# A sparse-and-dense key-value attention layer on one core: where the second dense pass of a tile stands

## What is computed

```python
x = x + relu(xn @ W_upd + (adj.T @ (xn @ W_msg)) / deg + bias)      # xn = layernorm(x)
q = (xn @ Wq) * 128 ** -0.5                                         # xn = layernorm(x) again
scores, index = product_keys(xn)            # top 16 of 128 on two sides, top 16 of the 256 sums
w = softmax(scores)                                                 # 16 weights per node and head
k = sum(w * keys_table[index]); v = sum(w * values_table[index])
x = x + softmax(causal(q @ k.T)) @ v @ Wo                           # 8 heads, float32
```

## Time and profile before

| what | value |
|---|---|
| time, median of 3 runs | 17072.46 us (17061.4 to 17086.94) |
| span of the profiled execution | 9595.0 us |
| that execution's own time outside its span | not given |
| median less span | 7477 us |
| PE busy | 8080.2 us, 84% |
| DVE busy | 7220.8 us, 75% |
| POOL busy | 6794.0 us, 71% |
| ACT busy | 4866.4 us, 51% |
| mean granted clock of TensorE | 0.888 |

### The profile page before, as it was taken

The page is one execution under the profiler, slowest core; times in us unless marked ns, Lnnn a source line. Parts: engine busy times, 40 slices in busy tenths (PEclk is TensorE's granted clock), DMA queues, the critical chain, the costliest instruction groups (busy, mean ns, idle before and its releaser), DMA issues.

```text
span 9595.0 us, 181229 instructions
## 1 busy us (share of the span) xinstructions
PE 8080.2 (84%) x51232; PEld 6240.2 (65%) x51232; DVE 7220.8 (75%) x32005; ACT 4866.4 (51%) x14163; POOL 6794.0 (71%) x7177
## 2 busy tenths in 40 slices
PE   5888888888888888888888888888888888888898
PEld 4666666666666766667666676666666666666676
DVE  7787777877777777777776777777777777877775
ACT  3555445455454554545445454454554545545454
POOL 5777767777677776777767777677776767767666
PEclk7899889998888998889888898898998989988898
DMA  4555445554454554545444454455554545545454
GB/s 126 166 171 161 155 154 162 163 162 158 155 160 158 162 165 150 160 157 166 158 152 158 159 164 157 155 162 161 164 165 150 166 151 165 167 150 160 146 167 138
DMA packets 445985, 1516.88 MB, mean 158 GB/s; under 512 B 123760, under 2 KB 141552, under 8 KB 379248
## 3 DMA queue, kind: packets, MB, share of 16 engines
q0 software_dynamic: 344064, 939.98, 32.5%
q1 hardware_dynamic: 100848, 564.37, 16.8%
HBM read 1499.66 MB, written 4.19 MB: 157 GB/s over the span
## 4 chain that ended last, share of the span: by engine, by line
PE 53%; DVE 36%; issue 5%; ACT 5%; DVEq 1%; DMA 0%; ACTq 0%; SPq 0%
PE dense_ps L470 20%; DVE wide L1114 10%; PE comb_ps L580 10%; PE wideT_ps L456 5%; PE front_ps L410 4%; DVE onehot L1005 4%; PE score_ps L446 4%; DVE chosen L1010 3%; DVE hits L1078 3%; DVE onehot L998 3%; PE score_ps L507 2%; PE score_ps L495 2%; PE probT_ps L513 2%; DVE neg L1131 1%; ACT expo L706 1%
## 5 line engine op out<-in xcount | busy, mean ns | idle before, releaser
L343 POOL DMA_INDIRECT got<-in_table,rows x7168 | 6792.1, 948 | 2778.2 <-issue 2203.5
L470 PE MATMUL dense_ps<-tab,wideT 128*128 128x256 f32 x16384 | 3959.9, 385 | 4.7 <-ACT kv_d L641 3.8
L470 PEld LDWEIGHTS dense_ps<-tab,wideT 128*128 128x128 f32 x16384 | 3002.5, 192 | 640.4 <-issue 274.7
L1114 DVE SCALAR_TENSOR_TENSOR wide<-const_ps,rank,expo 128x128 f32<-128x128 f32 x8192 | 2303.7, 344 | 1268.0 <-PE wideT_ps L456 993.1
L706 ACT ACTIVATE expo<-sim_d,shift 128x128 f32<-128x128 f32 x8192 | 2596.8, 393 | 118.0 <-DVE wide L1114 117.3
L641 ACT ACTIVATE wideT<-wideT_ps 128x512 f32<-128x512 f32 x2048 | 1212.0, 592 | 1070.2 <-PE wideT_ps L456 1065.8
L456 PE MATMUL wideT_ps<-ident,wide 128*128 128x128 f32 x8192 | 1237.1, 274 | 118.3 <-DVE wide L1114 61.0
L456 PEld LDWEIGHTS wideT_ps<-ident,wide 128*128 128x128 f32 x8192 | 1005.9, 141 | 386.0 <-DVE wide L1114 101.6
L580 PE MATMUL comb_ps<-got,spread 128*32 128x256 f32 x14336 | 1078.7, 452 | 4.8 <-DVEq L1102 4.0
L446 PE MATMUL score_ps<-group_of,lifted 128*128 128x16 f32 x1792 | 344.1, 329 | 554.3 <-DVE lifted L1021 554.3
L580 PEld LDWEIGHTS comb_ps<-got,spread 128*32 128x32 f32 x14336 | 481.5, 126 | 491.3 <-issue 299.5
(11 more groups left out here) (155 smaller groups left out, 8417.1 us busy)
## 6 DMA issues: line engine op xcount, KB each, us to landing
tab<-in_dense SPq DMA_DIRECT2D x512, 1024.0 KB
got<-in_table,rows POOLq DMA_INDIRECT x7168, 2.7
adj_i<-in_adj SPq DMA_DIRECT2D x16, 1024.0 KB, 9.6
x_in<-in_x SPq DMA_DIRECT2D x16, 256.0 KB
out<-fin SPq DMA_DIRECT2D x16, 256.0 KB, 6.0
tab<-in_wqpk_t SPq DMA_DIRECT2D x1, 512.0 KB, 11.0
tab<-in_keys_t SPq DMA_DIRECT2D x1, 512.0 KB, 15.5
wq_sb<-in_wq SPq DMA_DIRECT2D x1, 512.0 KB, 15.2
```

The costliest lines, as they stand in the source:

```text
L343: pool.indirect_dma_start(out=got[got_no(n)][:, g, :], out_offset=None, in_=table, in_offset=bass.IndirectOffsetOnAxis(ap=rows[:, t * GATH ...
L470: mm = pe.matmul(dense_ps[:, v * 2 * D:(v + 1) * 2 * D], wideT[k % 2][:, (2 * u + v) * P:(2 * u + v + 1) * P], tab[(k // CHUNK) % 2][:, (2 ...
L1114: last = dve.scalar_tensor_tensor(wide[k % 2][:, 2 * u + v, :], count_ps[:, v, :], rank1[:, 2 * half + v, key:key + 1], expo[k % 2][:, 2 * ...
```

## The change

The pass of place w[1] goes elsewhere on all three engines. On PE it stood between `key_transpose` and `scores` and now stands between `values` and `project`. On ACT it stood between the kv copy and `take_keyT` and now stands behind `take_headT`. On DVE it stood in front of the selection's second step and now stands behind w[4]. The plan's counts stay, so a slot has as many passes as before. DVE's `weigh` gets one wait more, at the first pass of each half: for its own last weighing, before the counts that this one reads are overwritten.

```diff
--- PE, batch
                 key_transpose(a, t, kv, kv_copied, slot + 1)
-                k = passes(b, k, w[1], first)
                 if t == 0:
                     pe.wait_ge(q_copied, s + 1)
...
                 values(a, t, kv)
+                k = passes(b, k, w[1], first)
                 project(a, h)
--- ACT, batch
                 copy(kv[:, t, :], comb_ps[:, 0:2 * D]).then_inc(kv_copied, 1)
-                k = passes(b, k, w[1], first, last)
                 take_keyT(a, t, keyT)
...
                 take_headT(a)
+                k = passes(b, k, w[1], first, last)
--- DVE, weigh
             if k % HALF_PASSES == 0:
+                dve.wait_ge(wide_ready, m)
                 after(link(dve.tensor_copy(count_ps, count_sb[:, :, :])))
--- DVE, batch
                 if half is not None and o == 2:
                     best_dense(half, 0)
-                k = passes(b, k, w[1], last)
                 hit_part(1)
...
                 k = passes(b, k, w[4], last)
+                k = passes(b, k, w[1], last)
                 if more and t % 2 == 1:
                     sum_rows(nt)
                     lift(m, t0, nt)
```

## The result

The changed kernel takes 16628.42 us (median of 4 runs, 16619.52 to 16643.95); beside it the kernel before took 17066.93. The ratio is 0.9742, 95% interval 0.9728 to 0.9756: 439 us less, where 194 had been forecast and 16710 was the low end of the range. The direction was right, the size not.

The account below looks back on a forecast made before the run. DVE was taken to set the end of odd slots, PE that of even ones. Gains of 150 + 4 + 40 = 194 us, with 7477 us outside the span held fixed, gave 17072 − 194 = 16878, say 16880; range 16710 to 17060.

Parts of the forecast that it names:

- the 7477 us: Gap between the profile's span of 9595 us and the median of 17072.46, taken as fixed and untouched by the change.
- step 3: Short slots n = 1, 2, 15, 16: moved pass against earlier negate, between 2 us less and 2 more each; taken as 0.
- Step 1: Even slots: PE's 0.37 us stall moves from project to scores; nothing gained, between 0 and 0.3 us worse per slot.
- Steps 2 and 4: Odd slots: DVE's wait for PE's turn goes, 10.0 us per batch; PE's clock drops less behind shorter waits, 2.6.
- the new wait that I looked for: Sign of being wrong: in odd slots DVE's moved weighing waits for PE's turn of w[4]; none expected in n = 9.
- Waits at the move: Sign of being right: PE's waits at L446 for DVE's lifted, 554.3 us in 194 waits, fall below 400 us.
- step 4: PE's clock after waits at the move: six places, a third helped, 2.6 us per batch, 40 us in all.
- rival (a): PE's clock stays up in all eight places, 204 us instead of 40: 16714 us; chance 0.12.
- rival (d): Slower: the moved pass runs at low clock in the four short slots, costing 222 us: 17197 us; chance 0.12.
- Step 5: POOL and DMA: POOL allows at most about 600 us of gain; added wait on wide_ready costs 10 us at most.
- (b): Rival: the gain scales with the timed run, 345 us instead of 194, giving 16727 us; chance 0.06.
- (c): Rival: DVE's new wait takes the old one's place, leaving 17072 us within 34; chance 0.12.

Follow-up runs that it names:

- e1: The kernel before, unchanged, run again for a second profile; 17248.99 us, with a span of 17247.1.
- e17: The kernel before with plain transfers from fixed places of the table instead of the 7168 gathers, run once more as a base; 9549.57 us.
- e18: The changed kernel with plain transfers from fixed places of the table instead of the gathers; 9246.72 us.
- e5: The whole changed kernel once more, beside the kernel before on one and the same chip; 16639.92 us, ratio 0.9747.
- e10: The changed kernel, but POOL waits after each 4 gathers until they have landed, all work done; 12698.38 us.

## Why the prediction was right and wrong

**The step that failed is the last of the sum**, the 7477 us: "I take this part as fixed". The trace of before was self-consistent and 7477 us short of every timed run; I treated the gap as a constant added behind the program. It was 44% of the time, inside the span, and the change acts on it. In e1 36% of the chain that ended last has no engine named, the mark of held signals; a forecast made on a profile without them can't see which handoffs cross a burst. The Trainium skill (Runtime: NRT & Kernel Launch, "The ~15µs preamble/postamble breakdown") leaves little room outside a kernel, and I had written what follows from it, that the rest would be the kernel's own time. That was right: 1.8 us lie outside here. The sum was 245 us short of the 439. Some 109 of them were missing in the steps themselves, nearly all in step 3, which I had put at 0, and 136 in this last one.

**How the 439 come about.** Without holds the change is worth 303 (e17, e18), with all the gathers 439 to 441. That leaves 136 to 138 us that are there with gathers and not with plain transfers. It isn't a sum that holds in between: with half the gathers the gain is 267, with a quarter nothing. By slot, in us per batch, with e1's slots scaled by the times of the kernel before on the two chips (an estimate, by 17080.79 / 17247.31 for e5 and 17066.93 / 17247.31 for the first profile of the changed kernel):

| slots | e1 to e5 | e1 to first profile after | e17 to e18 |
|---|---|---|---|
| odd, but 1 and 15 | −13.7 | −14.2 | −11.7 |
| 16 | −7.8 | −10.2 | −2.0 |
| 1, 2, 15 | −5.0 | −5.4 | −4.8 |
| the other even ones | −4.7 | −0.1 | −0.8 |

Of the 11 to 12 us a batch that the holds add, 6 to 8 are in the one slot n = 16. There `negate` comes 42.9 us behind the slot's start in e1 and at 22.0 in e5 (20.9 in the first profile after; medians of batches 1 to 14), and the slot lasts 54.1 us and then 40.5 (39.5). So scores and negate now get through the opening between the two rows of 16 gathers instead of waiting for the burst's end. n = 4 does the same in both traces, 42.8 and then 21.1 (22.0), 51.8 us and then 45.6 (45.7). n = 8 does so in e5 (45.5 us for 51.5), but not in the first profile after (51.1). That the opening is the reason is an argument from positions; no run isolates it.

**Step 1** was right without holds: n = 0, 4, 8, 12, 20 and 24 are within 0.25 us; n = 14 lost 1.6 and n = 6, 10, 18, 22 and 26 gained 0.4 to 0.7. The 0.37 us moved as told, from project to scores, as in the earlier trace rows. PE in slot 9 of e18:

```profile
4851.82 0.70 PE L492 MATMUL score_ps<-keyT,qT 128*128 128x256 f32 x2 [0.37 <-ACT keyT L638]
...
4857.60 0.63 PE L453 MATMUL wideT_ps<-ident,wide 128*128 128x128 f32 x4 [1.19 <-DVE wide L1112]
...
4863.06 0.39 PE L510 MATMUL probT_ps<-wo_sb,headT 128*128 128x128 f32 x2
4864.94 1.06 PE L443 MATMUL score_ps<-group_of,lifted 128*128 128x16 f32 x8 [1.49 <-DVE lifted L1018]
```

**Steps 2 and 4** had the right sum, 11.7 against 12.6, by compensating errors. I gave slot 9 1.0 us and it got 0.3; `lifted` starts 17.1 us behind the slot's start and not 16.4, and PE's 1.19 us wait for a weighing, which I had let go, is still there. DVE in slot 9 of e18, beside the earlier trace rows:

```profile
4852.19 1.12 DVE L1112 SCALAR_TENSOR_TENSOR wide<-const_ps,rank,expo 128x128 f32<-128x128 f32 x4
...
4856.40 1.12 DVE L1112 SCALAR_TENSOR_TENSOR wide<-const_ps,rank,expo 128x128 f32<-128x128 f32 x4 [1.01 <-ACT expo L703]
...
4860.72 1.13 DVE L1112 SCALAR_TENSOR_TENSOR wide<-const_ps,rank,expo 128x128 f32<-128x128 f32 x4 [0.16 <-PE wideT_ps L453]
...
4864.19 0.69 DVE L1018 TENSOR_TENSOR lifted<-const_ps,chosen 128x512 f32<-128x512 f32 x1
```

The wait for the turn is gone and the new wait that I looked for is 0.16 us; but the weighing of w[3] now waits 1.01 us for ACT's exponentials of w[2], 0.38 in the earlier trace rows. In this slot ACT takes a root behind keyT, with two table loads of 1.28 us, and these exponentials stand behind it; my working followed only turns. On the other side n = 5 and 25, to which I gave nothing, gained 1.5 and 1.6 us, and n = 3, 7 and 19 gained 1.7 to 2.1. DVE's waits for the turn fell from 987.1 to 438.8 us in all. Waits at the move fell from 554 to 440 us, not below 400. PE's busy time, for the same matmuls, fell by 93 us (8038.1 to 7945.2, granted clock 0.894 to 0.918) where step 4 had 40, though not only in the six places; rival (a) had 204.

**Step 3** was mis-sized: put at 0, it measured 6.9 us a batch, 103 in 15. My bound was 2 us less per slot; n = 1, 2, 15 and 16 gained 0.4, 1.2, 3.2 and 2.0. In n = 15 the wait for the probabilities hardly shrinks (5.05 us for 5.68, e17), but it ends 2.2 us earlier, and though `project`, behind the pass, starts 0.6 us later, it and the extra tile have the full clock: windows of slot 15 in e17 and in e18 (length, busy us by engine, granted clock), and PE's projection in each.

```profile
5124.21:5155.77 31.56, 21.09 (x101) 14.85 (x100) 21.89 (x89) 7.91 (x24) 1.96 (x4) 0.68 0.12 40
```

```profile
4962.56:4990.98 28.42, 19.54 (x101) 13.89 (x99) 21.50 (x87) 8.46 (x24) 1.38 (x3) 0.82 0.13 44
```

```profile
5141.56 0.79 PE L510 MATMUL probT_ps<-wo_sb,headT 128*128 128x128 f32 x2 [0.37 <-ACT headT L638]
```

```profile
4977.25 3.12 PE L467 MATMUL dense_ps<-tab,wideT 128*128 128x256 f32 x8
4980.20 0.60 PE L453 MATMUL wideT_ps<-ident,wide 128*128 128x128 f32 x4
4980.64 0.39 PE L510 MATMUL probT_ps<-wo_sb,headT 128*128 128x128 f32 x2
```

The pass begins at 1.2 GHz (3.12 us for eight multiplies that took 1.89 in its old place) and ends at 2.4; the projection takes 0.39 for 0.79, and the matmuls of the extra tile 0.49 for 0.79. I had priced the low clock as a cost of the moved pass, in rival (d); it brought the clock back. The granted clock of the slot rises from 0.68 to 0.82 here, from 0.76 to 0.88 in n = 16 and from 0.69 to 0.77 in n = 2; in n = 1, which gained least, it stays at 0.70 to 0.71.

**Step 5** was right in what it said: POOL isn't the bound, and DVE isn't idle ahead of the 32 count copies behind the added wait. (7168 × 1.248 is 8946, not 8990.) It left out what POOL's row of gathers does to PE's signals. **Rivals**: (a), at 16714, and (b), at 16727, lie nearest by their numbers, and neither is the cause. For (a) the clock gave too little. (b) fails since the gain doesn't go with the time: 303, −10, 267 and 441 us of gain at 9550, 9747, 12208 and 17081. (c) and (d) didn't come.

## What to carry to other kernels

Hold a profile's span against the timed median before anything else is read from it; where they differ, the profile is of another execution than the one to be made faster, and the gap is a term that any change may touch. Where GpSimd gathers with indirect transfers in long rows, try breaking the rows up: it took 24% off the changed kernel's time here (e10, a single run), against 2.6% for the change. And when a pass is moved on several engines, follow each thing that its consumer reads (exponentials too, not turns alone), and ask what the clock does behind a wait if work is put there.

## What the runs showed of the hardware that was not expected

- While GpSimd issues indirect gathers without a pause (one per 1.25 us), signals from TensorE reach ScalarE and VectorE late, nearly half of them at 4 to 6 us into the row and most from 6 us on; waits of up to 42.7 us end that way. Signals to two engines come at once (8024.16 and 8024.24 us). Of 393 moments at which holds of over 2 us end in e5, 188 fall in a pause of the row or behind its end, most of them 3 to 7 us behind the last issue, and 205 while the row goes on. Signals of ScalarE to TensorE took 0.05 us, 0.15 at most.
- An eighth of the bytes changes nothing (17125.9 us), four instead of any number under way neither (16531.48); plain transfers of the same bytes, issued by the same engine every 0.53 us, hold nothing (9574.78). A pause for the landing after each four gathers leaves few long holds (30 of 2684 handoffs over 3 us, 12698.38), one after each eight leaves holds of up to 21.9 us (14834.55). Whether the indices matter or the longer issue (948 ns against 537) isn't settled. The nearest thing that a page states is the warning in the Trainium skill (VectorE: DVE Perf Modes, "The TRN2 errata"), that increments of semaphores at a high rate by one engine can deadlock another. No run here shows a block that doesn't end, and the plain transfers made as many increments.
- Why the first profiled execution of the kernel before, at 9595 us and with all its gathers, had no holds, while every later one whose span is on record took 17058 us or more, stays open.
